# Three of four token groups get their sums of squares from VectorE, ScalarE and one-column products instead of Gram products on TensorE

## What is computed

```
attn = (w1 @ w2.T) * sparse_mask                  # 1024 x 1024
y    = gelu(x @ attn.T + b2)
z    = layernorm(x + y)                           # over the 1024 features of a token
e    = norm(z) > 64                               # per token: which table of weights
out  = layernorm(z + z @ W.T + bias)              # W from 4-bit codes and a table per row
```

## Time and profile before

| | |
|---|---|
| median of three runs | 307.38 us |
| span of the profiled execution, first to last instruction | 303.5 us |
| runs above that span | 3.5 to 4.1 us |
| PE busy | 289.2 us, 95% |
| DVE busy | 196.6 us, 65% |
| ACT busy | 183.9 us, 61% |
| POOL busy | 107.2 us, 35% |

### The profile page before, as it was taken

One profiled execution on the slowest core, in us unless ns is written; L12 is line 12 of the kernel. 1 busy time (PEld: TensorE's weight loads), 2 busy tenths in 40 slices (PEclk: granted clock), 3 DMA queues, 4 the chain that ended last, 5 costly groups with the idle time before them and its releaser, 6 DMA issues.

```text
span 303.5 us, 5064 instructions
## 1 busy us (share of the span) xinstructions
PE 289.2 (95%) x1907; PEld 253.9 (84%) x1907; DVE 196.6 (65%) x351; ACT 183.9 (61%) x244; POOL 107.2 (35%) x179
## 2 busy tenths in 40 slices
PE   7899998999999999999999999999999999999990
PEld 3788766666769999999999999999998888788780
DVE  2669998997868978898776785504135345344362
ACT  1965458988998967976986979341144453312210
POOL 4000002343344977798788200000033333323321
PEclk9999999999999999999999999999999999999996
DMA  6999999999999301111101111119237875444223
GB/s 222 398 355 356 377 383 294 247 260 227 207 193 200 87 21 37 35 37 35 37 35 38 52 45 44 54 36 257 91 129 250 265 253 199 172 153 158 104 101 118
DMA packets 28480, 49.78 MB, mean 164 GB/s; under 512 B 2464, under 2 KB 11936, under 8 KB 28448
## 3 DMA queue, kind: packets, MB, share of 16 engines
q1 hardware_dynamic: 23536, 40.79, 38.9%
q0 software_dynamic: 4352, 8.39, 15.4%
q10 hardware_dynamic: 560, 0.20, 0.3%
HBM read 36.79 MB, written 12.58 MB: 163 GB/s over the span
## 4 chain that ended last, share of the span: by engine, by line
PE 78%; SPq 7%; DVE 5%; DMA 3%; ACT 2%; issue 2%; POOL 1%; POOLq 0%; DVEq 0%
PE acc L559 20%; PE acc L561 19%; PE acc L560 19%; PE acc L542 5%; PE acc L488 4%; DMA w<-in_w2d 3%; PE acc L463 2%; SPq L273 2%; PE acc L498 2%; PE acc L465 2%; PE acc L464 2%; SPq L272 1%; SPq L277 1%; PE acc L430 1%; PE acc L475 1%
## 5 line engine op out<-in xcount | busy, mean ns | idle before, releaser
L559 PE MATMUL acc<-lin,zz 128*128 128x256 f32 (+2 forms) x424 | 130.3, 307 | 0.3 <-issue 0.3
L561 PE MATMUL acc<-lin,zz 128*128 128x256 f32 (+2 forms) x424 | 129.9, 306 | 0.0
L560 PE MATMUL acc<-lin,zz 128*128 128x256 f32 (+2 forms) x424 | 129.7, 306 | 0.0
L559 PEld LDWEIGHTS acc<-lin,zz 128*128 128x128 f32 x424 | 80.1, 189 | 4.6 <-issue 0.5
L560 PEld LDWEIGHTS acc<-lin,zz 128*128 128x128 f32 x424 | 80.3, 189 | 4.0
L561 PEld LDWEIGHTS acc<-lin,zz 128*128 128x128 f32 x424 | 80.2, 189 | 4.1
L724 ACT ACTIVATE leaf<-planes,lut,flip 128x1024 f32<-128x1024 uint8 x56 | 67.5, 1239 | 1.3 <-DVE dest L992 1.3
L992 DVE COPY_PREDICATED leaf<-planes,leaf 128x1024 f32<-128x1024 uint8 x32 | 43.4, 1358 | 12.7 <-ACT leaf L724 11.9
L1377 POOL DMA_DIRECT2D z<-in_xr x16 | 19.5, 1221 | 71.0 <-ACT z L706 69.6
L827 ACT ACTIVATE junk<-rows,cols 128x1024 bf16<-128x1024 f32 x15 | 17.2, 1150 | 41.6 <-POOL cols L1351 41.6
L1349 POOL TENSOR_TENSOR cols<-cols 128x1 f32<-128x1 f32 x15 | 9.5, 633 | 77.7 <-DVE rows L1112 77.7
(11 more groups left out here) (108 smaller groups left out, 430.9 us busy)
## 6 DMA issues: line engine op xcount, KB each, us to landing
z<-in_xt SPq DMA_DIRECT2D x16, 512.0 KB, 8.8
z<-in_xr POOLq DMA_DIRECT2D x16, 512.0 KB, 8.3
out_rows<-rows SPq DMA_DIRECT2D x15, 512.0 KB, 2.9
out_rows<-parts SPq DMA_DIRECT2D x32, 128.0 KB, 1.7
rows<-out_rows SPq DMA_DIRECT2D x16, 256.0 KB, 2.6
w<-in_w1d SPq DMA_DIRECT2D x7, 512.0 KB, 9.0
off_band<-in_mask_rest SPq DMA_DIRECT2D x8, 448.0 KB, 4.1
w<-in_w2d SPq DMA_DIRECT2D x3, 584.0 KB, 9.4
```

The source lines that it names most:

```text
L559: nc.tensor.matmul(bank, hi, w_hi, start=k == 0, stop=False)
L560: nc.tensor.matmul(bank, hi, w_lo, start=False, stop=False)
L561: last = nc.tensor.matmul(bank, lo, w_hi, start=False, stop=k == KB - 1)
```

## The change

The Gram products stay for the four tiles of group 0 only. For groups 1 to 3, DVE adds the two parts of z (`make_whole`, 128x1024, four times a group), ACT squares each sum (`square_whole`), DVE adds the four squares up (`add_squares`, three times) and folds the two halves (`fold_squares`, 128x512); PE then sums over partitions with four one-column products in fp32 (`group_squares`) and DVE copies the four columns (`read_sums`). POOL makes only the mean of each tile in the first stage (`tile_mean1`) and the statistics of a group at once, on four columns (`group_statistics1`).

Group 1's sums stand ahead of the last stage on DVE. Those of groups 2 and 3 stand in it, `SUM_STEPS`, behind `add_bias(j, 1)` of tiles 1 to 9. PE's one-column products stand behind its tiles 1, 6 and 10, the reading and the statistics behind tiles 2, 6 and 10, and `find_high` moves behind the statistics of tile 10. The decode's steps are spread anew over the first two stages, 65 in all as before.

```
-    FIRST_STEPS = [2, 2, 2, 1, 2, 2, 2, 1, 2, 2, 2, 2, 3, 2, 3, 2]
-    SECOND_STEPS = [2] * 15 + [3]
+    FIRST_STEPS = [2, 2, 2, 1, 1, 2, 1, 2, 1, 2, 2, 2, 2, 2, 2, 2]
+    SECOND_STEPS = [3, 2, 2, 3, 2, 2, 2, 3, 2, 2, 2, 3, 2, 2, 2, 3]
+    GRAM_TILES = PER_GROUP
+    SQUARES_BEHIND = {1: 1, 6: 2, 10: 3}
+    STATISTICS_BEHIND = {2: 1, 6: 2, 10: 3}
+    SUM_STEPS = {1: ((2, 0),), 2: ((2, 1),), 3: ((2, 2), (2, 3)), 4: ((2, 4), (2, 5)), 5: ((2, 6), (2, 7)),
+                 6: ((3, 0), (3, 1)), 7: ((3, 2), (3, 3)), 8: ((3, 4), (3, 5)), 9: ((3, 6), (3, 7))}
...
+            def group_squares(g):
+                pe.wait_ge(squares_added, PAIRS * g)
+                for c in range(PER_GROUP):
+                    last = nc.tensor.matmul(acc[:, SQUARE_BANK[g], c:c + 1], square_sum[:, c * P:(c + 1) * P], one_col,
+                                            start=True, stop=True)
+                last.then_inc(gram_done, 1)
...
-                if STATS_AHEAD <= j + 1 < TILES:
+                if STATS_AHEAD <= j + 1 < GRAM_TILES:
                     tile_squares(j + 1)
...
+            def square_whole(g, r):
+                n = PAIRS * (g - 1) + r
+                act.wait_ge(whole_made, n + 1)
+                part = whole[WHOLE_IN[r]][:, :, :]
+                nc.scalar.activation(part, part, ACT.Square).then_inc(squared1, 1)
...
+                nc.vector.tensor_tensor(whole[WHOLE_IN[r]][:, :, :], zz[:, 0, g, pair, :].bitcast(f32),
+                                        zz[:, 1, g, pair, :].bitcast(f32), ALU.add).then_inc(whole_made, 1)
...
                 add_bias(j, 1)
+                for g, n in SUM_STEPS.get(j, ()):
+                    sum_step(g, n)
+                if j in STATISTICS_BEHIND:
+                    read_sums(STATISTICS_BEHIND[j])
...
             for j in range(TILES):
-                tile_statistics1(j)
-            pool.wait_ge(rstd1, TILES)
-            find_high(slice(0, TILES), norm_step, 0, high_made)
+                tile_mean1(j)
+            group_statistics1(0)
             for j in range(LAST):
                 if j:
                     rstd_of_tile2(j - 1)
                 mean_of_tile2(j)
+                if j in STATISTICS_BEHIND:
+                    group_statistics1(STATISTICS_BEHIND[j])
+                    if STATISTICS_BEHIND[j] == GROUPS - 1:
+                        pool.wait_ge(rstd1, GROUPS)
+                        find_high(slice(0, TILES), norm_step, 0, high_made)
```

More of the change, by code:

```diff
@@ L125, in post_ln_block @@
         parts = at("parts", 160.25, [8, WIDE], f32)
+        whole = [at(f"whole{n}", kib, [2, GROUP], f32) for n, kib in enumerate((160.25, 196.3125, 164.28125))]
+        square_sum = at("square_sum", 194.3125, [GROUP], f32)
         leaf = at("leaf", 168.3125, [4, D], f32)
@@ L220, in post_ln_block @@
         gram_done, squares_read = sem("gram_done"), sem("squares_read")
-        var1, rstd1 = sem("var1"), sem("rstd1")
+        mean1, var1, rstd1 = sem("mean1"), sem("var1"), sem("rstd1")
+        whole_made, squared1, squares_added = (sem(n) for n in ("whole_made", "squared1", "squares_added"))
         mean2, squared2, var2_made, rstd2_made = (sem(n) for n in ("mean2", "sq2", "var2m", "rstd2m"))
@@ L505, in turn @@
                 elif b == KB - 1:
-                    pe.wait_ge(squares_read, TILES)
+                    pe.wait_ge(squares_read, GRAM_TILES)
                 elif b > 1:
@@ L620, in _ @@
                     linear_part(j, 2, 2).then_inc(tile_done, 1)
+                if j in SQUARES_BEHIND:
+                    group_squares(SQUARES_BEHIND[j])
             pe.wait_ge(bad_made, 1)
@@ L838, in _ @@
             make_lin_hi(LAST_PAIR)
+            square_whole(1, 0)
+            square_whole(1, 1)
             make_lin_hi(LAST_PAIR + 1)
+            square_whole(1, 2)
+            square_whole(1, 3)
             for j in range(LAST):
@@ L843, in _ @@
                 square2(j)
+                for g, n in SUM_STEPS.get(j, ()):
+                    if n in WHOLE_STEPS:
+                        square_whole(g, WHOLE_STEPS.index(n))
             act.wait_ge(flag_made, 1)
@@ L1102, in add_bias @@
                 if h == 0:
-                    dve.wait_ge(rstd1, j + 1)
+                    dve.wait_ge(rstd1, j // PER_GROUP + 1)
                     if j == 0:
@@ L1132, in tile_squares, with make_whole, add_squares, fold_squares @@
                 read_squares(GRAM_BANKS[j % 2], zsq[:, j:j + 1], squares_read)
+            def make_whole(g, r):
+                if (g, r) == (1, 0):
+                    for slot in range(4):
+                        dve.wait_ge(spilled[slot], 16 * (EARLY_PARTS // 8))
+                if (g, r) == (1, 2):
+                    for slot in range(4, 8):
+                        dve.wait_ge(spilled[slot], 16 * (EARLY_PARTS // 8))
+                if r == 0 and g > 1:
+                    dve.wait_ge(squares_added, PAIRS * (g - 1))
+                elif r == 3:
+                    dve.wait_ge(squares_added, PAIRS * (g - 1) + 1)
+                pair = slice(2 * r, 2 * r + 2)
+                nc.vector.tensor_tensor(whole[WHOLE_IN[r]][:, :, :], zz[:, 0, g, pair, :].bitcast(f32),
+                                        zz[:, 1, g, pair, :].bitcast(f32), ALU.add).then_inc(whole_made, 1)
+            def add_squares(g, r):
+                dve.wait_ge(squared1, PAIRS * (g - 1) + r + 1)
+                if r > 1:
+                    dve.wait_ge(squares_added, PAIRS * (g - 1) + r - 1)
+                total = whole[0][:, :, :]
+                nc.vector.tensor_tensor(total, total, whole[WHOLE_IN[r]][:, :, :], ALU.add).then_inc(squares_added, 1)
+            def fold_squares(g):
+                dve.wait_ge(squares_added, PAIRS * g - 1)
+                if g > 1:
+                    dve.wait_ge(gram_done, GRAM_TILES + g - 1)
+                nc.vector.tensor_tensor(square_sum[:, :], whole[0][:, 0, :], whole[0][:, 1, :], ALU.add).then_inc(
+                    squares_added, 1)
+            def sum_step(g, n):
+                if n in WHOLE_STEPS:
+                    make_whole(g, WHOLE_STEPS.index(n))
+                elif n == 7:
+                    fold_squares(g)
+                else:
+                    add_squares(g, (3, 5, 6).index(n) + 1)
+            def read_sums(g):
+                dve.wait_ge(gram_done, GRAM_TILES + g)
+                nc.vector.tensor_copy(zsq[:, PER_GROUP * g:PER_GROUP * (g + 1)],
+                                      acc[:, SQUARE_BANK[g], 0:PER_GROUP]).then_inc(squares_read, 1)
             for j in range(STATS_AHEAD):
@@ L1143, in _ @@
                 done = decode_steps(SECOND_STEPS[j], done)
+            sum_step(1, 0)
+            sum_step(1, 1)
             make_lin_lo(LAST_PAIR)
+            sum_step(1, 2)
+            sum_step(1, 3)
             make_lin_lo(LAST_PAIR + 1)
+            for n in range(4, 8):
+                sum_step(1, n)
             def last_part(n):
@@ L1337, in statistics1, with tile_mean1, group_statistics1 @@
                 pool.wait_ge(step, before + 4)
-            def tile_statistics1(j):
-                c = slice(j, j + 1)
-                pool.wait_ge(squares_read, j + 1)
+            def tile_mean1(j):
                 pool.wait_ge(saved, j + 1)
-                statistics1(c, parts[:, j % 8, QUARTER:QUARTER + 1], var1, 4 * j)
+                nc.gpsimd.tensor_scalar(mean[:, j:j + 1], parts[:, j % 8, QUARTER:QUARTER + 1], 1.0 / D, None,
+                                        ALU.mult).then_inc(mean1, 1)
+            def group_statistics1(g):
+                c = slice(PER_GROUP * g, PER_GROUP * (g + 1))
+                if g == 0:
+                    pool.wait_ge(squares_read, GRAM_TILES)
+                    pool.wait_ge(mean1, TILES)
+                else:
+                    pool.wait_ge(squares_read, GRAM_TILES + g)
+                nc.gpsimd.tensor_tensor(mean_sq[:, c], mean[:, c], mean[:, c], ALU.mult).then_inc(var1, 1)
+                nc.gpsimd.tensor_scalar(var[:, c], zsq[:, c], 1.0 / D, None, ALU.mult).then_inc(var1, 1)
+                pool.wait_ge(var1, 4 * g + 2)
+                nc.gpsimd.tensor_tensor(var[:, c], var[:, c], mean_sq[:, c], ALU.subtract).then_inc(var1, 1)
+                pool.wait_ge(var1, 4 * g + 3)
+                nc.gpsimd.tensor_scalar(mean_sq[:, c], var[:, c], EPS, None, ALU.add).then_inc(var1, 1)
+                pool.wait_ge(var1, 4 * g + 4)
                 nc.gpsimd.tensor_tensor(rstd[:, c], mean_sq[:, c], neg_halves[:, c], ALU.pow).then_inc(rstd1, 1)
```

4 lines of the change are left out of this document (3 added, 1 removed).

## The result

The changed kernel took 308.69, 310.88, 310.78 and 309.88 us, a median of 310.33, against 307.5 us for the kernel before in four runs on the same chip. The ratio is 1.0102, with a 95% interval of 1.0077 to 1.0126: about 1% slower. The forecast was 310.0 us.

The account below looks back on a forecast made before the run. PE bounds the kernel up to the last stage, then a DVE, POOL, ACT ring of 4.73 us a tile. 208.1 + 66.2 + 18.0 = 292.3, 2.6 us later, gives 310.0 us; range 306.6 to 313.0.

Parts of the forecast that it names:

- Twelve Gram products less: First two stages: 11.4 us off PE, so t0 (start of tile 0's second bias half on DVE) falls from 219.2 to 208.1.
- turn 3: PE's turn before the last stage, where the decode might not keep up: wait of 0.3 us taken, range 0 to 3.
- rival 4: The decode falls behind by 3 us at the turns and everything shifts, 313 us; chance 0.07.
- One-column products: On PE: eight narrow fp32 matmuls per group take 0.9 us, three groups 2.6 us; bounds 0.4 to 2.5 us a group.
- POOL held by the sums: Last stage: POOL's mean waits for DVE's sums; +1.3 us at tiles 3, 4, 7, 8, +0.8 at 1, 5, 9.
- Rival 2: Sums beside the mean don't delay it in the last stage; t14 = 282.7, 300.4 us; chance 0.10.
- rival 3: POOL is held through a run of DVE instructions: 2.2 instead of 1.3 in five tiles, 314.5 us; chance 0.10.
- The statistics and the power: POOL in the last stage: +2.0 us at tile 2, +2.8 at tile 6, +5.6 at tile 10 with find_high.
- rival 1: POOL's power on sixteen columns is short, some 0.6 to 1.4 us; t14 about 289.5, 307.4 us; chance 0.20.
- The sum: Last-stage additions of 18.0 us; t14 (start of tile 14's second bias half on DVE) at 292.3 against 289.7, 2.6 later.
- PE: Last stage: PE waits 5.3 us for group 2's fold, a 4 us low clock loses 2 us, tile 14 ends at 288.5.
- The median: Whole kernel: 2.6 us later, added to 307.4, gives 310.0 us; what follows t14 was taken as alike in both kernels.

Follow-up runs that it names:

- the PSUM operand: Against the changed kernel, DVE's sums of groups 2 and 3 read one operand from PSUM instead of SBUF, values meaningless; 302.24 us, ratio 0.9831 to the kernel before.

## Why the forecast came true

**Twelve Gram products less.** Forecast was t0 at 208.1 with 0.3 us of wait at turn 3; it came at 208.64 with 0.22. Of the 0.5 us between, 0.37 were there ahead of all that was changed: PE's first Gram products start at 91.66 instead of 91.29. The decode did not fall behind (rival 4), and the experiment with the old spread gives the same t0.

**One-column products.** Forecast 0.9 us a group; the eight of group 3 took 0.95 in one row:

```profile
266.65 0.95 PE L603 MATMUL acc<-cols,square_sum 128*128 128x1 f32 x8
```

**POOL held by the sums.** Shown, by the PSUM operand: same DVE time, no hold, t14 8.9 us sooner. The forecast steps above 4.73 were 1.3 and 0.8; measured were 1.35 at tiles 3, 4, 7 and 8 and 0.9 at 1, 5 and 9. Rival 2 (no hold) and rival 3 (held through a run of DVE instructions) are both refuted by the rows of tile 4: POOL is held to the end of the instruction in which it starts, and let in between two that stand back to back. The Trainium skill ("SBUF — State Buffer", "Who interferes with whom") names as contending a VectorE instruction with two SBUF inputs beside a GpSimd one that reads SBUF, and that is what the PSUM operand takes away here; the runs agree.

**The statistics and the power.** Forecast 1.0 us for a power on four columns and 2.9 on sixteen, read out of a row of 4.04 by taking off the time in which it was held. Measured 1.04 and 2.92, the second with DVE idle beside it. So 1.1 us of the 4.04 in the earlier trace rows were waiting, and rival 1 (a short power) is refuted. Tiles 2 and 6 lengthened by 1.7 and 2.7 against 2.0 and 2.8; tile 10 by 5.5 against 5.6, of which leaving `find_high` out takes 4.6 back.

**The sum.** Additions in the ring 18.1 us measured against 18.0; t14 at 292.97 against 292.3. Of the 0.7 us between, 0.5 are t0's. That the additions meet within 0.1 us is in part luck: tiles 2, 6 and 10 came 0.5 us under the forecast together, and the seven tiles with sums alone as much over it.

**PE.** Forecast was a wait of 5.3 us (measured 5.34) and a low clock of 4 us. The low level lasted 6.8 us, PE was busy in 6.2 of them, and at half speed that is an estimated loss of 3.1 us instead of 2.0. With a fold that came 0.6 us later than forecast (240.3 against 239.7), PE's tile 14 ended at 290.2 instead of 288.5. The 4 us had a weak source. The nine matmuls of the earlier trace rows took 0.45 us each, where one of 512 columns later takes a step of 0.24, and that was read as the low level; but the stretches that they lie in show a granted clock of 1.00, so the row alone doesn't show how long a low level lasts. One of them, from the kernel before:

```profile
2.00:4.00 2.00, 2.00 (x6) 0.76 (x5) 0.00 (x0) 1.49 (x2) 1.62 (x5) 1.00 0.91 289
```

The length of the low level is the one term that was mis-sized by much, and it cost nothing in the kernel after because the ring is later still. It is not without weight, though: with `find_high` out, PE's tiles set t14 at 290.51, and the gain stops at 2.5 us instead of 4.6.

**The median.** 310.33 against 310.0. The forecast added 2.6 to the median; the spans of the two profiles differ by 3.4, the medians by 2.8, and the changed kernel's runs by 2.2 among themselves. Behind t14, where the prediction took both kernels to be alike, the profiles are not all alike. In each of them DVE's last instruction ends 9.3 to 9.4 us behind t14, but the span ends 13.8 us behind it in the kernel before, 13.9 in the changed one, and up to 17.3 in the experiments. Most of the difference is in SP's issue of the last two stores, here in the changed kernel and then in the one with PE's products later:

```profile
301.89 0.92 SPq L375 DMA_DIRECT2D out_rows<-rows  x2
```

```profile
301.61 3.74 SPq L375 DMA_DIRECT2D out_rows<-rows  x2
```

Why these differ, no run shows, and with one profile a kernel it is only likely, not shown, that the runs of one kernel differ by the same. The two profiles compared here have the same end, so their 3.4 us and the 3.3 of t14 are the better measure of the change, and the forecast was some 0.7 us low; that the median came within 0.3 is in part luck. In the experiments t14 compares better than single spans.

**What the steps did not foresee.** With the hold gone (the PSUM version), tile 5 still took 5.7 us. ACT's row there, the same view:

```profile
234.96 0.95 ACT L841 ACTIVATE off_band<-off_band 128x896 f32<-128x896 f32 x1 [2.63 <-DMA off_band<-in_mask_rest]
...
235.91 1.14 ACT L852 ACTIVATE junk<-rows,cols 128x1024 bf16<-128x1024 f32 x1
```

A sum for the flag waits for its DMA and stands ahead of the squares of the tile, though POOL had that tile's mean at 234.44, 1.5 us earlier than the squares began: once the ring is fast, the next thing in it is ACT's queue.

What stays open is what sets how long the clock stays low once PE is busy again: 6.8 us in the kernel after, 10.2 with `find_high` out, after waits of the same 5.3 us. No experiment changed that alone.

## What to carry to other kernels

Spare time on an engine is not spare time in a ring: before work is moved onto VectorE, look for the small GpSimd instructions that run beside it and that something waits for, and cost each at the rest of the VectorE instruction in which it would start. Place such sums behind those small instructions, one at a time, or feed one operand from PSUM. Work that "nothing waits for" stays cheap only where it stands; queued ahead of a per-tile instruction it costs its full length once, here 4.6 us.

## What the runs showed of the hardware

- The same tensor_tensor on 128x1024 took VectorE 1.22 us with two SBUF operands and with one in PSUM, but only the first held GpSimd (its two instructions took 1.11 and 1.09 us against 0.19 and 0.23).
- GpSimd's power took 0.57, 1.04 and 2.92 us for 1, 4 and 16 columns on 128 partitions; adds and products took about 0.2 on all three widths.
- The hold is one-sided as far as these runs show: beside the power of the earlier trace rows, whose own 2.92 us can only have begun in that pair, VectorE's pair took the 2.86 us of the earlier trace rows; a like pair, beside which GpSimd's instructions only ended behind VectorE's, took 2.83. The page of the Trainium skill named above says that the other side blocks while GpSimd has the ports; here the measurement differs. Whether GpSimd holds the ports through the whole of a power, no run shows. VectorE's like pair:

```profile
158.03 2.83 DVE L992 COPY_PREDICATED leaf<-planes,leaf 128x1024 f32<-128x1024 uint8 x2 [1.17 <-ACT leaf L724]
```

- After a wait of PE of 5.3 us the granted clock was at half (1.2 GHz) for 6.8 us in one kernel and 10.2 in another, though PE was busy for all but the first 0.6 and 2.8 us of it.
